# Expert stage: every first-layer product over 128 tokens written as two over 64 tokens each

## The reference, cut to what matters

```
h = silu(x_e @ w1[e] + b1[e])      # 512 -> 2048 features
y = h @ w2[e] + b2[e]              # 2048 -> 512 features
out += gate_weight * y             # for the tokens that picked expert e
```

## Time and profile before

| what | us |
|---|---|
| time of the two runs | 1468.13 and 1470.18, median 1469.16 |
| profiled execution, span from its first to its last instruction | 1469.3 |
| matmul busy in that span | 1237.3 (84%) |
| weight loads busy | 848.8 (58%) |
| VectorE busy / ScalarE busy / GpSimd busy | 1016.8 / 761.8 / 298.5 |
| first first-layer matmul of the expert stage | at 986.05 |
| last second-layer matmul of the expert stage | at 1454.86 |

### The profile page before, as it was taken

One profiled execution on the slowest core, in us unless ns is written; L12 is line 12 of the kernel. 1 busy time (PEld: TensorE's weight loads), 2 busy tenths in 40 slices (PEclk: granted clock), 3 DMA queues, 4 the chain that ended last, 5 costly groups with the idle time before them and its releaser, 6 DMA issues.

```text
span 1469.3 us, 33539 instructions
## 1 busy us (share of the span) xinstructions
PE 1237.3 (84%) x12366; PEld 848.8 (58%) x12367; DVE 1016.8 (69%) x1663; ACT 761.8 (52%) x1227; POOL 298.5 (20%) x363
## 2 busy tenths in 40 slices
PE   3735799998588999847489999768999999999996
PEld 2205576775466677423345555636677677767674
DVE  3668888888788888869567667475567755476432
ACT  2236577677666767622643424424466655375331
POOL 0121223332222333422000000034111111111111
PEclk9766999999899999979599999658999999999998
DMA  4043000003200000320220000328347564446111
GB/s 147 1 155 123 13 5 5 5 3 115 69 12 6 5 4 4 104 119 11 97 115 0 0 0 0 134 107 254 136 143 250 191 201 136 143 168 219 24 26 22
DMA packets 38129, 120.26 MB, mean 82 GB/s; under 512 B 9960, under 2 KB 14184, under 8 KB 28080
## 3 DMA queue, kind: packets, MB, share of 16 engines
q1 hardware_dynamic: 32416, 107.28, 20.3%
q0 software_dynamic: 5648, 12.13, 4.1%
HBM read 105.61 MB, written 12.76 MB: 81 GB/s over the span
## 4 chain that ended last, share of the span: by engine, by line
PE 47%; DVE 4%; ACT 2%; issue 2%; POOL 0%; POOLq 0%; DVEq 0%; ACTq 0%
PE banks L2349 16%; PE banks L2370 15%; PE banks L1880 7%; PE banks L1910 3%; PE banks L2319 1%; PE banks L2302 1%; PE banks L1936 1%; PE banks L2336 1%; PE banks L1949 1%; ACT ab_wi_hi L1749 1%; PE banks L2295 1%; PE banks L1959 1%; DVE f_qa L1418 0%; PE banks L1933 0%; ACT ab_un L1783 0%
## 5 line engine op out<-in xcount | busy, mean ns | idle before, releaser
L2349 PE MATMUL banks<-eb_x_hi,eb_w_hi 128*128 128x128 f16 x1344 | 228.7, 220 | 4.7 <-DVE eb_w_lo L2229 4.7
L2349 PE MATMUL banks<-eb_x_lo,eb_w_hi 128*128 128x128 f16 x1344 | 228.6, 220 | 0.0
L2349 PE MATMUL banks<-eb_x_hi,eb_w_lo 128*128 128x128 f16 x1344 | 228.6, 220 | 0.0
L1118 PE MATMUL banks<-mb_u_hi,mb_wi_hi 128*128 (+3 forms) x1088 | 190.7, 221 | 12.4 <-ACT mb_ca L845 10.7
L1118 PE MATMUL banks<-mb_u_hi,mb_wi_lo 128*128 (+3 forms) x1088 | 190.4, 221 | 0.0
L1118 PE MATMUL banks<-mb_u_lo,mb_wi_hi 128*128 (+3 forms) x1088 | 190.2, 221 | 0.0
L2229 DVE TENSOR_TENSOR eb_w_lo<-eb_raw,eb_w_hi 128x2048 f32 (+1 forms) x64 | 142.6, 2287 | 23.0 <-ACT eb_w_hi L2235 16.0
L647 DVE SCALAR_TENSOR_TENSOR mb_ca<-mb_xp,mb_par,mb_ca 128x128 f32<-128x128 f32 x384 | 149.5, 451 | 5.2 <-ACT mb_ca L845 3.4
L2349 PEld LDWEIGHTS banks<-eb_x_hi,eb_w_hi 128*128 128x128 f16 x1344 | 132.4, 99 | 7.4 <-issue 5.1
L2349 PEld LDWEIGHTS banks<-eb_x_lo,eb_w_hi 128*128 128x128 f16 x1344 | 132.4, 98 | 2.4
L2349 PEld LDWEIGHTS banks<-eb_x_hi,eb_w_lo 128*128 128x128 f16 x1344 | 132.4, 99 | 0.0
(11 more groups left out here) (441 smaller groups left out, 2842.6 us busy)
## 6 DMA issues: line engine op xcount, KB each, us to landing
eb_raw<-e_w SPq DMA_DIRECT2D x64, 1024.0 KB, 6.0
mb_ring<-m_in_w SPq DMA_DIRECT2D x8, 1072.0 KB, 6.5
ab_raw<-a_in_w SPq DMA_DIRECT2D x4, 1154.0 KB, 9.0
mb_ring<-m_out_w SPq DMA_DIRECT2D x4, 1024.0 KB, 5.3
xcm<-x_cm SPq DMA_DIRECT2D x4, 512.0 KB, 5.1
t_res<-x_tm SPq DMA_DIRECT2D x1, 2048.0 KB, 8.9
t_kept<-t_res SPq DMA_DIRECT2D x8, 256.0 KB, 2.0
mb_wi_hi<-t_kept SPq DMA_DIRECT2D x1, 2048.0 KB, 9.2
```

The costliest lines, as they stand in the source:

```text
L1118: x = e.matmul(ps[0:width, bank, n * P:(n + 1) * P], a[:, k, f:f + width], b[:, k, ds(i * P, P)], start=(k == 0 and m == 0), stop=(k == KD ...
L2349: o = e.matmul(ps[:, j, c * P:(c + 1) * P], a[:, side, k, f * P:(f + 1) * P], b[:, k, :], start=(k == 0 and m == 0), stop=(k == KD - 1 and ...
```

## The change

Each output tile's 12 matmuls over 128 tokens become 12 over the first 64 tokens and then 12 over the last 64. The weights, the sums and the places in the PSUM bank stay the same. Each 128 x 128 weight piece is now loaded twice, since every matmul has a load of its own. A block executes 384 first-layer matmuls and as many loads, and a turn of a loop holds 768 of each, for the two sides.

```diff
+HALF = P // 2
...
                 for c in range(EX_GB):
                     f = j * EX_GB + c
-                    for k in range(KD):
-                        for m, (a, b) in enumerate(((w_hi, x_hi), (w_hi, x_lo), (w_lo, x_hi))):
-                            o = e.matmul(ps[:, j, c * P:(c + 1) * P], a[:, side, k, f * P:(f + 1) * P], b[:, k, :],
-                                         start=(k == 0 and m == 0), stop=(k == KD - 1 and m == 2))
+                    for n in range(0, P, HALF):
+                        for k in range(KD):
+                            for m, (a, b) in enumerate(((w_hi, x_hi), (w_hi, x_lo), (w_lo, x_hi))):
+                                o = e.matmul(ps[:, j, c * P + n:c * P + n + HALF], a[:, side, k, f * P:(f + 1) * P],
+                                             b[:, k, n:n + HALF], start=(k == 0 and m == 0), stop=(k == KD - 1 and m == 2))
                 o.then_inc(h_mm, 1)
```

## The result

The changed kernel took 1498.23 us (two runs, 1495.60 and 1500.86) against 1469.16 before: a ratio of 1.0183 with a 95% interval of 1.0159 to 1.0208. 1479.5 us was forecast. The direction was right and the time lies inside the range, but the loss is 29 us and not the 10.4 of the sum.

What follows compares the result with a forecast made beforehand. TensorE alone was taken to bound the expert stage. The one term, 4032 split products x 2.57 ns = +10.4 us on the profiled 1469.3, gave 1479.7, stated as 1479.5 us (+0.7%); range 1446 to 1501 us.

Steps and rivals of the forecast that it cites:

- the sum: Over all split first-layer products: 4032 x 2.57 ns = +10.4 us, all on the path.
- What bounds the kernel: Expert stage: TensorE alone sets the pace, so a longer or shorter first layer shows in full, 21 times.
- The price of 64 columns: First layer: a 64-column matmul with its load costs 29.2 ns, two 58.4 ns, 2.57 ns more than one of 128.
- The floor at 25.05 ns: Least time of a load and matmul pair, from a run of 96 with 32 columns; it binds below 54 columns.
- the line above it: Matmul price fitted through 128 and 512 columns: 0.416 ns a column plus a fixed 2.57 ns.
- Rival 1: First layer: a 64-column pair costs only 26.6 or 25.05 ns, so 10.4 or 23.2 us faster; chance 0.14.
- What else is touched: Other engines' waits, transfers, PSUM sums and the first block's clock: at most a fraction of a microsecond changes.
- rival 2: Expert loops: code outgrows TensorE's store, turns pay 4.39 us; about half of 19 cost 40 us, all 83; chance 0.15.
- the range's upper end: 1501 us: the forecast plus 22 us, for about five turns that pay 4.39 us, or slow issue.
- The cover: The queue of loads and matmuls before TensorE hides the doubled issue; without it a pair costs 25.05 ns, under 29.2.
- the start of the second loop: No idle time at 1343.08 was taken to show that the jump before side 1's first layer is covered.
- Rival 3: First layers: short matmuls let the clock fall to 0.50, 108 instead of 56 ns a product, +210 us; chance 0.03.

Runs made afterwards that it cites:

- e12: The changed kernel with each product cut at 96 and 32 columns instead of 64 and 64; 1533.14 us, ratio 1.0416.
- e1: The changed kernel measured again without an edit; 1498.50 us, ratio 1.0188 to the kernel before.
- e8: The changed kernel with either half's matmuls taking all 128 columns, so each first layer is computed twice; 1692.31 us in a single run.
- e4: The changed kernel with one loop over the blocks on TensorE instead of two; 1486.25 us, ratio 1.0107 to the kernel before.
- e5: The kernel before, 128 columns, plus 192 never-run loads and matmuls behind either first-layer copy, under a condition the build can't decide; 1497.18 us, ratio 1.0206.
- e13: Half of the change: groups 0 and 1 of a first layer with 64 columns, 2 and 3 with 128; 1478.99 us, ratio 1.0056.
- e11: The changed kernel with 32 columns in four passes, 768 loads and matmuls in a first layer; 1875.53 us in a single run.
- e9: The kernel before with one loop over the blocks and one copy of the first layer, its side in a register; 1539.47 us, ratio 1.0470.
- e3: The kernel before with one loop over the blocks on TensorE instead of two; 1466.68 us, ratio 0.9969.

## Why the prediction was right in its price and wrong in its sum

**What bounds the kernel** was right: TensorE alone, in full, 21 times, and after the change no line of another engine has more than 0.4% of the chain that ended last.

**The price of 64 columns** was right to the tenth of a nanosecond: 29.2 ns, 22.03 us a block. The floor at 25.05 ns and the line above it were tested at 96 and 32 columns (e12) and hold. Rival 1 falls.

**The sum** failed. It had one term, 4032 x 2.57 ns, and by "What else is touched" nothing was to be added. The term that is missing is the code that each loop fetches in its first turns, with the lower clock behind the stops: 14 us in the profiled execution, by the medians some 18 (16 in e1). I had the mechanism before me in rival 2, with the price of a stop (2.5 and 6.9 us), but as one question with two answers, the code stays or it doesn't; and the answer "it stays" was given a cost of nothing. It does stay, for 1640 loads and matmuls, in the changed kernel's later turns. But each loop must fetch it first, nearly twice as much of it, and the changed kernel stopped for that in four blocks where the kernel before stopped in two. That the time still lies inside the range is owed to the range's upper end, which stood for five turns that pay 4.39 us; since other turns paid, and other amounts, this was in part luck.

**The cover** was the other step that failed. I wrote that the queue of loads and matmuls in front of TensorE covers the doubled issue, and that without it a pair costs 25.05 ns. Fetches have to be covered too, and that I left out. e8 shows it: in block 17 the same program fetches the same six packets in the same time each, and loses 9.0 us with matmuls 29.2 ns apart and 3.7 with matmuls 55.9 ns apart; none of its stops lies inside a first layer. That the cover is made of matmuls still to be done, and lasts half as long when these are halved, is my reading; no run shows how far ahead of TensorE the fetches run. I also took the start of the second loop as a sign that a jump ahead of a first layer is covered. Block 17 makes its jump behind the first layer, so it was no such sign, and at the head of block 20 TensorE stood 1.87 us.

That the second loop's copy of the code is a part of the loss is shown by e4 (12.3 us). The length of the code by itself is less clear: at the old pace and with the same jumps it costs 2.4 us in block 19 and nothing in sum (e8), in e5, with a jump more, 26 us. In the changed kernel the longer code and the faster passage act together.

**Rival 2's price per turn** was wrong for this size: not 9 to 19 turns pay, but four (1, 2, 17 and 19), all among the first of a loop. **Rival 3** falls: the granted clock is 1.00 in every undisturbed block; in blocks 2 and 17 it drops behind the stops, to 0.88 and 0.94 on average.

**Open.** It is not shown why block 2 fetches again, on a path that block 1 has just run, while e8 and e13 fetch nothing there. Which code is kept and which is dropped as a loop fills the store is not shown: e5 and the changed kernel hold the same 1640 loads and matmuls in a turn and stop in different blocks. Whether a stop takes longer while weights are being loaded was not tried. The Trainium skill ("Runtime: NRT & Kernel Launch", "Instruction fetch mechanics") gives TensorE room for 2048 instructions; 1640 staying in the changed kernel and 3176 not staying in e11 agree with that, the late stops of e5 at 1640 don't follow from the number alone.

## What to carry to other kernels

Halving the columns of a matmul with its own weight load costs the fixed part once more, here 2.57 ns, as long as the columns stream longer than the floor, here 25 ns; a line through two sizes of the same kernel's trace gives this. But count the code too: here more instructions in a loop's body were paid in the first turns of every copy of the loop, most of all at jumps, and the shorter matmuls hid less of it. A second copy of a large loop body, here for the turns beyond a fixed count, costs its own fetches: one loop instead of two gained 4.9 us in the kernel before and 12.3 in the changed one.

## What was not expected of the hardware

The floor of one load and one matmul is the same at 32 columns within a stream of 96-column ones as in a run of 96 alone: 25.3 ns in e12 against 25.05. Register operations in front of loads are dear: 64 pairs of them made a first layer of e9 3.8 us longer (14.44 against 10.67 us), about 59 ns a pair. And the same program's time varied by 18 us between runs in e5 (59 packets, 1491.74 to 1509.74), but by 4 us with one loop in e3 (35 packets); the changed kernel in e1, with 54 packets, varied by 6.7, so the number of fetches alone does not set the spread.
